# Attention scores as three split products with remainders from GpSimd, and rows of the shared stage turned through DRAM in five batches

## The reference, cut to what matters

```python
# cross attention, in fp32
q = (queries @ Wq + bq).reshape(B, L, H, dk)          # B 8, L 512, H 16, dk 16
k = (keys @ Wk + bk).reshape(B, S, H, dk)             # S 64
scores = einsum('blhd,bshd->bhls', q, k)
scores = where(triu(ones((L, S)), k=1), -inf, scores)
attn = softmax(scores / sqrt(dk)); out = attn @ v; x = x + out @ Wo + bo
# shared expert and router, on xf = layernorm(x)
shared = new_gelu(xf @ Wfc_s + bfc_s) @ Wproj_s + bproj_s     # 256 -> 1024 -> 256
probs = softmax(xf @ Wr); topk_p, topk_i = top_k(probs, 2)
```

## Time and profile before

| what | value |
|---|---|
| median of 3 runs | 917.37 us (916.71 to 919.8) |
| the profiled execution's own time | 916.98 us |
| its span | 915.3 us |
| TensorE busy | 886.2 us, 97% |
| VectorE, ScalarE, GpSimd busy | 625.2, 524.0, 331.0 us |
| mean granted TensorE clock | 0.991 |

### The profile page before, as it was taken

One profiled execution on the slowest core, in us unless ns is written; L12 is line 12 of the kernel. 1 busy time (PEld: TensorE's weight loads), 2 busy tenths in 40 slices (PEclk: granted clock), 3 DMA queues, 4 the chain that ended last, 5 costly groups with the idle time before them and its releaser, 6 DMA issues.

```text
span 915.3 us, 20404 instructions
## 1 busy us (share of the span) xinstructions
PE 886.2 (97%) x6734; PEld 778.9 (85%) x6743; DVE 625.2 (68%) x1465; ACT 524.0 (57%) x1050; POOL 331.0 (36%) x318
## 2 busy tenths in 40 slices
PE   8999998999998999999999999999999999999996
PEld 6688995566554888888988999999999999999996
DVE  5998696899877776666656766575665657575553
ACT  4683434556455655446444775575766667575552
POOL 3477222211302555555553224232232323322222
PEclk9999999999999999999999999999999999999998
DMA  9300020000002111111226556335353533533332
GB/s 251 121 1 1 2 92 1 2 1 1 1 7 94 51 54 67 66 61 67 84 95 224 141 114 145 47 54 128 48 131 47 139 47 47 139 47 47 47 47 35
DMA packets 87855, 64.00 MB, mean 70 GB/s; under 512 B 58112, under 2 KB 80832, under 8 KB 87680
## 3 DMA queue, kind: packets, MB, share of 16 engines
q0 software_dynamic: 17504, 34.87, 16.5%
q1 hardware_dynamic: 60192, 26.80, 11.5%
q10 hardware_dynamic: 10112, 1.70, 1.1%
HBM read 38.58 MB, written 24.77 MB: 69 GB/s over the span
## 4 chain that ended last, share of the span: by engine, by line
PE 79%; DVE 7%; DMA 4%; ACT 4%; issue 4%; POOL 1%; SPq 0%; ACTq 0%; DVEq 0%; POOLq 0%
PE PS L137 22%; PE PS L139 21%; PE PS L138 21%; DMA metar<-routed_rows 3%; PE PS L894 3%; PE PS L309 2%; PE PS L924 2%; PE PS L938 1%; PE PS L944 1%; ACT hideh L1913 1%; DVE mxpad L1138 1%; PE PS L1402 1%; ACT act32e L1915 1%; PE PS L1384 1%; DMA win<-in_W_inT 1%
## 5 line engine op out<-in xcount | busy, mean ns | idle before, releaser
L1944 POOL DMA_INDIRECT out_rows<-y,toki x70 | 113.5, 1622 | 265.9 <-DVE y L1974 246.6
L1913 ACT ACTIVATE hideh<-PS,be 128x256 fp32r<-128x256 f32 x280 | 143.7, 513 | 101.3 <-PE PS L139 101.2
L143 DVE TENSOR_TENSOR hidel<-act32e,hideh 128x256 fp32r<-128x256 f32 x280 | 118.0, 425 | 84.0 <-ACT act32e L1915 81.6
L137 PE MATMUL PS<-xTeh,wfch 128*128 128x256 f32 x560 | 158.6, 283 | 1.9 <-ACT act32e L1915 1.1
L137 PE MATMUL PS<-wprh,hideh 128*128 128x256 f32 x560 | 158.5, 283 | 1.9 <-DVE hidel L143 1.9
L138 PE MATMUL PS<-xTel,wfch 128*128 128x256 f32 x560 | 157.6, 281 | 0.0
L139 PE MATMUL PS<-xTeh,wfcl 128*128 128x256 f32 x560 | 157.5, 281 | 0.0
L139 PE MATMUL PS<-wprh,hidel 128*128 128x256 f32 x560 | 156.5, 279 | 0.0
L138 PE MATMUL PS<-wprl,hideh 128*128 128x256 f32 x560 | 156.3, 279 | 0.0
L1915 ACT ACTIVATE act32e<-PS,be 128x256 f32<-128x256 f32 x280 | 144.6, 516 | 8.7 <-DVE hidel L143 8.1
L137 PEld LDWEIGHTS PS<-wprh,hideh 128*128 128x128 f32 x560 | 104.9, 187 | 5.2 <-DVE hidel L143 4.9
(11 more groups left out here) (273 smaller groups left out, 2059.8 us busy)
## 6 DMA issues: line engine op xcount, KB each, us to landing
xb<-routed_rows SPq DMA_DIRECT2D x144, 64.0 KB
fcraw<-in_Wfc POOLq DMA_DIRECT2D x8, 1024.0 KB, 6.0
prraw<-in_Wproj POOLq DMA_DIRECT2D x8, 1024.0 KB, 9.0
out_rows<-X SPq DMA_DIRECT2D x8, 512.0 KB, 2.9
X<-in_x SPq DMA_DIRECT2D x7, 512.0 KB, 7.6
routed_rows<-pads SPq DMA_DIRECT2D x8, 272.0 KB, 4.3
out_rows<-y,toki POOLq DMA_INDIRECT x70, 3.8
ctx<-in_ctxT SPq DMA_DIRECT2D x4, 256.0 KB, 7.1
```

What stands on the lines that cost most here:

```text
L137: nc.tensor.matmul(out, wh, xh, start=first, stop=False)
L143: return eng.tensor_tensor(out, whole, high.bitcast(F32), ALU.subtract)
L1913: nc.scalar.activation(hid[0][:, j, :], PS[:, j % 4, 0:BLK], ACT.Gelu_apprx_tanh, bias=bias)
L1944: nc.gpsimd.indirect_dma_start(out=out, out_offset=bass.IndirectOffsetOnAxis(ap=toki[:, h:h + 1], axis=0), in_=y[:, h, :], in_offset=None, ...
```

## The change

In the attention stage qT becomes a pair: ScalarE copies each half of the queries twice, into qT's high part and, in fp32, into one buffer q32; GpSimd subtracts (`q_low`). GpSimd also splits the keys of each batch (`split_keys`) into a double buffer of pairs. Row scores and key scores become three fp32r matmuls for each one of fp32. The remainders of the shared weights move from VectorE to GpSimd (`weight_low`). Of VectorE's apply_part(b+3) the last two tiles move into the next iteration, behind its first maximum.

In the shared stage, batches 2 to 6 are no longer turned by TensorE: SyncE writes the normalised rows hn to DRAM and reads them back in four DMAs of 32-column squares (`quarters`), and VectorE turns them (`turn`) from SBUF into PSUM. The order of the work in the period before such a batch is another one (`whole_turned`). Batches 0, 1 and 7 keep TensorE's transposes, with columns permuted as hn is written; the weights Wfc_s and Wr are permuted on the host to match.

```diff
-            qT = old("qT", [P, 2, KD, L])
+            qT = [old("qTh", [P, 2, KD, L], F32R), Place(w_at)("qTl", [P, 2, KD, L], F32R)]
+            q32 = Place(yD_at + 3 * pair_bytes)("q32", [P, L])
+            PARTS = ((0, 0), (0, 1), (1, 0))
 def row_scores(b, t):
                     pe.wait_ge(qT_ready, KD * b + KD)
+                    pe.wait_ge(k_split, 2 * b + 2)
                     for m in range(KD):
-                        for half in range(2):
+                        for n, (qp, kp) in enumerate(PARTS):
+                            for half in range(2):
+                                last = nc.tensor.matmul(
+                                    at, qT[qp][rows, b % 2, m, t * P:(t + 1) * P],
+                                    kpair[b % 2][kp][rows, m, :].rearrange("p (i n) -> p i n", i=2),
 def key_scores(b, m):
-                    for j in range(NG):
-                        nc.tensor.matmul(PS[:, j, :], kbd[rows, b, m, j % 2 * P:(j % 2 + 1) * P],
-                                         qT[rows, b % 2, m, :], start=True, stop=False, skip_group_check=True)
+                    for n, (qp, kp) in enumerate(PARTS):
+                        for j in range(NG):
+                            nc.tensor.matmul(PS[:, j, :], kpair[b % 2][kp][rows, m, j % 2 * P:(j % 2 + 1) * P],
+                                             qT[qp][rows, b % 2, m, :], start=n == 0, stop=False,
+                                             skip_group_check=True)
 def evac_q(b, m):
-                    nc.scalar.activation(qT[:, b % 2, m, :], PS[:, q_bank(b, m), :], ACT.Identity,
-                                         bias=bq[:, m:m + 1]).then_inc(qT_ready, 1)
+                    nc.scalar.activation(qT[0][:, b % 2, m, :], PS[:, q_bank(b, m), :], ACT.Identity,
+                                         bias=bq[:, m:m + 1])
+                    if b + m:
+                        act.wait_ge(qT_ready, KD * b + m)
+                    nc.scalar.activation(q32[:], PS[:, q_bank(b, m), :], ACT.Identity,
+                                         bias=bq[:, m:m + 1]).then_inc(q_high, 1)
+                def split_keys(b):
+                    if b >= 2:
+                        pool_wait(pool, s_psum, 2 * NG * (b - 1))
+                    kh, kl = kpair[b % 2]
+                    nc.gpsimd.tensor_copy(kh[:], kbd[:, b]).then_inc(k_split, 1)
+                    pool_wait(pool, k_split, 2 * b + 1)
+                    low(nc.gpsimd, kl[:], kbd[:, b], kh[:]).then_inc(k_split, 1)
+                def q_low(b):
+                    for m in range(KD):
+                        pool_wait(pool, q_high, KD * b + m + 1)
+                        low(nc.gpsimd, qT[1][:, b % 2, m, :], q32[:], qT[0][:, b % 2, m, :]).then_inc(qT_ready, 1)
                 pool_wait(pool, bo_ready, 1)
+                split_keys(0)
+                q_low(0)
+                split_keys(1)
                 add_bo(0)
                 for b in range(1, B):
                     if b + 1 < B:
                         rstds(b + 1)
+                    q_low(b)
+                    if b + 1 < B:
+                        split_keys(b + 1)
                     add_bo(b)
+                    if b < 5:
+                        weight_low(b - 1)
 attention_vector, iteration b
                     maxima(b + 1, 0)
+                    if behind and after:
+                        for t in pair(1):
+                            apply_part(b + 2, t)
-                    if 0 < b < 5:
-                        low(nc.vector, parts[1][:, part], whole[:, part], parts[0][:, part]).then_inc(ws_low, 1)
                     if b + 3 < B:
-                        for t in range(TB):
+                        for t in pair(0):
                             apply_part(b + 3, t)
 shared stage
+            DIRECT = (0, 1, B - 1)
+                def quarters(b):
+                    sp.wait_ge(hn_ready, b + 1)
+                    sp.dma_start(HN.rearrange("(t p) d -> p t d", p=P), hn[:]).then_inc(xq_in, 16)
+                    sp.wait_ge(xq_in, XQ_IN * (b - FIRST) + 16)
+                    for q in range(P // SQ):
+                        sp.dma_start(xq[q * SQ:(q + 1) * SQ].rearrange("p t k i -> p t (k i)"),
+                                     HN[:, q * KD * SQ:(q + 1) * KD * SQ].rearrange("(t j) c -> j t c", j=SQ))...
                 for b in range(B - 2):
+                    if b + 2 not in DIRECT:
+                        quarters(b + 2)
                     store(b)
+                def turn(b):
+                    dve.wait_ge(xq_in, XQ_IN * (b - FIRST + 1))
+                    dve.wait_ge(lT_ready, b)
+                    nc.vector.transpose(PS[:, 4:4 + KD, :].rearrange("p k (t j) -> p t k j", j=SQ),
+                                        xq[:]).then_inc(hT_psum, 1)
+                def whole_turned(b, first=2):        # TensorE
+                    up(b, range(first, KH))
+                    down(b, range(1))
+                    logits(b + 1)
+                    down(b, range(1, 2))
+                    transpose_logits(b + 1)
+                    down(b, range(2, TB))
+                    ranks(b + 1)
+                    up(b + 1, range(2))
+                def whole_turned(b, first=2):        # ScalarE
+                    gelus(b, range(first, 6))
+                    evac(b + 1)
+                    gelus(b, range(6, KH))
+                    ...
+                    evac_logits(b + 1)
+                    copy_rows(b + 1)
+                    gates(b + 1)
+                    gelus(b + 1, range(2))
+                def place(b):                        # VectorE
+                    place_rows(b)
+                    lows(b, range(1))
+                    for m in range(2):
+                        place_slots(b, m)
+                    lows(b, range(1, 2))
+                    place_gates(b)
+                def whole_turned(b, first=2):
+                    lows(b, range(first, 4))
+                    stats_part(b + 2)
+                    lows(b, range(4, 5))
+                    turn(b + 1)
+                    lows(b, range(5, 6))
+                    x_low(b + 1)
+                    lows(b, range(6, KH))
+                    apply_part(b + 2)
+                    choose(b + 1)
+                    residual(b, range(2))
+                    place(b + 1)
 TensorE and ScalarE
                 for b in range(1, B):
-                    whole(b)
+                    (whole if b + 1 in DIRECT + (B,) else whole_turned)(b)
```

More of the change, by code:

```diff
@@ L165, in build @@
         ident16 = ab("ident16", [P, P], BF16)
+        yD_at = ab.at
         yD = ab("yD", [P, KE * L])
@@ L890, in row_scores @@
                     for m in range(KD):
-                        for half in range(2):
[L892 to L899, removed]
+                        for n, (qp, kp) in enumerate(PARTS):
+                            for half in range(2):
+                                rows = slice(half * P // 2, (half + 1) * P // 2)
+                                at = PS[:, 4 + half, :].rearrange("p (i m n) -> p i m n", i=2, m=KD)[:, :, m, :]
+                                end = m == KD - 1 and n == len(PARTS) - 1
+                                last = nc.tensor.matmul(
+                                    at, qT[qp][rows, b % 2, m, t * P:(t + 1) * P],
+                                    kpair[b % 2][kp][rows, m, :].rearrange("p (i n) -> p i n", i=2),
+                                    start=m + n == 0, stop=t > 0 and end, skip_group_check=True)
+                                if t and end:
+                                    last.then_inc(n_psum, 1)
                     if t == 0:
@@ L1505, in copy_rows @@
                         act.wait_ge(scattered, 16 * 2 * TB * b)
-                    nc.scalar.activation(rows[:, :, 0:D], hn[:], ACT.Copy).then_inc(hn_copied, 1)
+                    if b in DIRECT:
+                        for t in range(TB):
+                            last = nc.scalar.activation(
+                                rows[:, t, 0:D].rearrange("p (q k i) -> p q k i", k=KD, i=SQ),
+                                hn[:, t, :].rearrange("p (k q i) -> p q k i", k=KD, i=SQ), ACT.Copy)
+                    else:
+                        last = nc.scalar.activation(rows[:, :, 0:D], hn[:], ACT.Copy)
+                    last.then_inc(hn_copied, 1)
                 def gates(b):
@@ L1620, in apply_part, with apply_permuted @@
                     dve.wait_ge(hn_rstd, 2 * b + 2)
-                    norm_apply(b).then_inc(hn_ready, 1)
+                    (apply_permuted if b in DIRECT else norm_apply)(b).then_inc(hn_ready, 1)
+                def apply_permuted(b):
+                    for t in range(TB):
+                        last = nc.vector.tensor_scalar(
+                            hn[:, t, :].rearrange("p (k q i) -> p k q i", k=KD, i=SQ),
+                            X[:, TB * b + t, :].rearrange("p (q k i) -> p k q i", k=KD, i=SQ), mv[:, t, 0:1],
```

(2 more changed lines are left out.)

43 lines of the change are left out of this document (33 added, 10 removed).

## The result

Run side by side, the changed kernel's median is 934.99 us (934.37 to 936.21, 4 runs), that of before 918.3 us (916.71 to 919.8, 4 runs): a ratio of 1.0197, with an interval of 1.0174 to 1.022. The changed kernel is 2% slower. The profiled execution took 935.44 us, its span is 933.8 us and its granted clock 0.986 (0.991 before).

The account below looks back on a forecast made before the run. It took TensorE's work as the bound, while what other engines hand it comes early. The profiled 916.98 us, attention +6.7 and shared stage +14.5 gave 938.2; with 0.4 for the median, 938.5 us, range 921 to 955.

Parts of the forecast that it names:

- Split scores on TensorE: Attention: three fp32r matmuls for each fp32 one save TensorE 7.2 us together, 0.90 in each iteration.
- p: Attention: time of one GpSimd subtraction of 128x512 with two inputs, taken as 1.8 us, between 1.40 and 2.10.
- part 2: Attention: the queries' longer way back to TensorE through copies and GpSimd subtractions; loop +1.8 us, opening +4.9.
- 223.82 + 2p: Attention loop: time the queries reach TensorE, which is there at 226.33; a wait of 1.1 us at p of 1.8.
- VectorE held back: Attention loop: GpSimd's reads delay VectorE's division and remainders, taken as 0.3 us an iteration; loop +1.8 us in all.
- The weights' remainders: Attention loop: moving them from VectorE to GpSimd costs nothing, GpSimd's work being covered with 0.9 us left.
- Transposes: Shared stage: eight transposes removed from TensorE save 0.79 us in each of five periods, 4.0 us.
- Turn at 9.2, down late by 2.5: Shared stage: VectorE's transposition is done 9.2 us into the period, so TensorE's first down tile ends 2.5 us late.
- The loop over sent rows and choose, period 27.9: Shared stage: sending rows, copying, normalising, then a contended choose delay ranks, making the period 27.9 us against 24.89, +3.0.
- B: Rival: choose without contention, and queries at p = 1.4 with the opening at 3.3; about 923 to 930 us, chance 0.17.
- A: Rival, faster: neither way is reached and TensorE's 7.2 + 4.0 us fall out whole; 906 us, chance 0.10.
- C: Rival, the clock: stalls in the shared periods and attention's waits lower the granted clock; 948 to 955 us, chance 0.13.

Follow-up runs that it names:

- e11: e1 with GpSimd subtracting each half of the queries' remainder twice, the second time over the first: 959.24 us, ratio 1.0476.
- e12: e1 with the weights' remainders back on VectorE as before the change: 922.5 us, ratio 1.0078.
- e6: e1 with VectorE normalising tiles 0 and 1 of the batch after next ahead of the last maxima: 920.78 us, ratio 1.0044.
- e9: e1 with the edits of e6 and e7, and GpSimd's weights' remainders moved right behind the next iteration's queries' remainders: 923.71 us, ratio 1.0086.
- e5: Changed kernel with both moves in VectorE's order of the turned batches, those of e3 and e4: 922.51 us, ratio 1.0065.
- e3: Changed kernel with VectorE's transposition right behind remainders 2 and 3, and the statistics behind remainder 7: 941.14 us, ratio 1.027.
- e1: Kernel before with the attention part of the change alone: 919.52 us, ratio 1.0049.
- e7: e1 with the first two batches' query remainders done by VectorE in one instruction each, without second copy or GpSimd: 919.02 us, ratio 1.0024.
- e2: Kernel before with the shared-stage part of the change alone: 931.93 us, ratio 1.0167.
- e4: Changed kernel with choose ahead of the normalising of the batch after next in VectorE's turned batches: 932.44 us, ratio 1.0205.

## Why the prediction was right, and which terms were not

The forecast was 938.5 us; measured 934.99. The likeliest case held, with both mechanisms and their places. Of the signs named beforehand all came in kind but one: the first row score was to start 2.4 to 3.6 us after the key score and started 1.67 us after it (213.13 and 211.46), with GpSimd's qTl as what ended the wait.

- **Split scores on TensorE (-7.2 us).** Half right. The row halves and groups do run side by side. A row score went from 1.06 us to 0.91 from its start to the next step, 0.15 saved (0.14 forecast). The second key score with what is added to it went from 1.53 to 1.48 us, 0.05 and not 0.16. From its start to the first product of the mask it did fall by 0.17 (211.38 to 212.69 before, 217.55 to 218.69 after); but the next row score begins 0.34 us behind that product and not 0.22, for a reason that wasn't looked into. Four times 0.15 and twice 0.05 is 0.7 an iteration; 0.57 of it shows in the busy time, where 0.90 stood in the sum. By the Trainium skill's rule of loads that last their columns over 1.2 GHz ("TensorE: Matmul & The Clock Gate", LDWEIGHTS), a load of 128 columns is 107 ns. Taken one after another, twelve make an estimate of 1.28 us to the next step; the trace has 0.91 and rules out that order.
- **p, GpSimd's subtraction (1.8 us).** The mis-sized term of part 2. It took 1.26 to 1.34 us in the opening and 1.28 to 1.34 in the loop, below even my lower bound of 1.40, which was twice the 0.70 us of a 256-column add. The formula 223.82 + 2p was right (e11). With 1.3 it gives a wait of 0.1 for the 1.1 in the sum; 0.25 was measured. In the opening, 128.3 + 3p gives 132.2 at 1.3, before row score (0,0) at 133.65: the copy of the keys took 1.85 us where I had 0.9. Key score (0,0) came out +3.96 against +4.9 (at p = 1.26, 149.2 + 2p and the row score's 1.67 give 153.4; 153.19 was measured).
- **VectorE held back (+1.8 in the loop).** Right in kind, and not found in full. Behind ScalarE's second copy the copy of the maxima comes later, so VectorE's split of them waits 0.68 us (229.18) where it waited 0.17; then division, normalising and outputs' remainders lie beside GpSimd, the normalising of two tiles at 1.70 us. That is the new wait of 0.33 for oTl. In all: the six iterations that had +0.2 and +0.3 each in the sum, 3.0 together, took 0.47 less than before. The first had nothing but a saving in the sum and took 1.8 more, largely by the clock. Attention: +3.5 for +6.7, within its -2 to +13.
- **The weights' remainders (nothing).** Not contradicted (e12 gains nothing by taking them back); e6 and e9 show that the cover I named is thin.
- **Transposes (-4.0).** With both waits gone (e5) a period is 0.49 us shorter than before, where 0.79 stood; the other 0.3 was not looked into, beyond a wait of 0.14 us at down.
- **Turn at 9.2, down late by 2.5.** It ended 9.1 us into the period; 2.17 measured. (The sum behind it comes to 23.63 and not 23.65; the 2.93 that follows is two up blocks, 2.78, and 0.15 that the text doesn't name.)
- **The loop over sent rows and choose, period 27.9.** 27.37, 27.37 and 27.38 us in three periods, of which the contended choose is part (409.14 to 413.83, 4.7 us), and 28.17 in one with a clock of 0.55 in 376:378, 0.8 us for the clock. Shared stage +15.0 for +14.5. Counted between the starts of up (j = 0), batch 1 cost 3.1 for 2, at a clock of 0.66 in 347:352; batches 2 to 5 10.7 for 12; the whole(6) behind them 1.2 for 0.5. So the sum's near hit is in part luck: terms that were too high stand against others too low and a clock that it left out. e3 to e5 show that both waits are real and lie side by side, as the sum treated them.
- **Rivals.** B needed a choose without contention: it was contended. A needed turn before 6.7. C's mechanism is real here, in three places of the profiled run: the first attention iteration, the period of batch 1 and the one behind it. Together that is far from C's 10 us and more, and the mean clock is 0.986 for 0.991, so C is not the case; e11 shows what it costs once the waits are over 4 us.

Against the profiled execution the sum was 938.2 for 935.44: 3.2 us too much in attention, 0.5 too little in the shared stage. Of the 3.2 us, 0.9 is the opening, where p was too high. The loop as a whole is 1.3 us later for the 1.8 in the sum. The remaining 1.8 is luck: the clock behind the loop, low in the profiled run of before and full in the changed kernel's, which was no term of mine.

## What to carry to other kernels

Work moved to an idle engine still sits on a way: count copy, subtract, copy, subtract through one buffer from the producer to TensorE, and double a step to see whether the way binds. Where two ways of like length run in parallel, removing one shows little or a loss; remove both before judging either. Before comparing the starts of an instruction in two runs, take them from a common point just ahead of the edited stage: 2 of the 3.9 us between e1 and e7 were older than the edit. Before placing a long GpSimd instruction on SBUF, list what VectorE does on SBUF at that time and who awaits it.

## What the runs showed of the hardware beyond the forecast

- VectorE and GpSimd can hold each other back on SBUF until the other's instruction ends: a 0.19 us copy took 1.04 and two remainders 3.77 instead of 1.28 us, ending 0.06 and 0.55 us behind GpSimd's; GpSimd's subtraction took 2.04 instead of 1.30 beside VectorE's normalising (e11), and one of its sends 1.47 instead of 0.96 (e3). The Trainium skill ("SBUF — State Buffer", SBUF: two separate sides) has the two engines share a pair of ports that one of them holds for a whole instruction, a VectorE operation with two SBUF inputs among them; these runs agree. VectorE's maxima, read from PSUM beside GpSimd, stayed at 1.19 to 1.23 us in the seven runs read.
- GpSimd's cost with two inputs grows less than in proportion to the columns: 0.70 us for 256 (a mean of four adds), 1.26 to 1.34 for 512, 2.37 to 2.39 for 1024.
- Short waits inside dense work can bring the clock down too, though not each time. Behind waits of 1.6 to 1.8 and 0.5 us at down the granted clock stayed at 1.00 in seven of twelve turned periods (three of four in the changed kernel, two of four each in e2 and e4). Behind one of 2.7 to 3.2 us at ranks it stayed in one of four (e3, else 0.57 to 0.78), and behind one of 4.1 to 4.8 us in none of six (e11, 0.50 to 0.66). That idle time costs more in one piece than in several is likely, but the first two counts are too small to show it.
